# A head's row of score maxima written by one DMA from columns of every fourth query, without a transpose

## The reference

```python
# block 0: q = tgt @ Wq.T, k = memory @ Wk.T, v = memory @ Wv.T, 16 heads of 32
probs = jax.nn.softmax(einsum('bhqd,bhkd->bhqk', q, k) * scale, axis=-1)
att = einsum('bhqk,bhkd->bhqd', probs, v)
x = tgt + att[0]
# block 1, x (8, 512, 512), y (8, 512, 512)
q = layer_norm(x) @ Wq;  k, v = split(layer_norm(y) @ Wkv)
o = softmax(q k^T * 32 ** -0.5) v
x = x + o @ Wproj + bproj
x = x + gelu(layer_norm(x) @ W1 + b1) @ W2 + b2
```

## Time and profile before

| | us |
|---|---|
| median of 3 runs | 1885.43 |
| lowest and highest of them | 1879.63, 1895.04 |
| the profiled execution | 1889.92 |
| its span in the trace | 1888.1 |
| TensorE (PE) busy | 1750.5 (93%) |
| mean granted TensorE clock | 0.972 |

### The profile page before, as it was taken

One profiled execution on the slowest core, in us unless ns is written; L12 is line 12 of the kernel. 1 busy time (PEld: TensorE's weight loads), 2 busy tenths in 40 slices (PEclk: granted clock), 3 DMA queues, 4 the chain that ended last, 5 costly groups with the idle time before them and its releaser, 6 DMA issues.

```text
span 1888.1 us, 23894 instructions
## 1 busy us (share of the span) xinstructions
PE 1750.5 (93%) x7488; PEld 1339.1 (71%) x7488; DVE 1094.3 (58%) x1860; ACT 1166.9 (62%) x1935; POOL 935.6 (50%) x778
## 2 busy tenths in 40 slices
PE   6899999887898899999999999999999999999898
PEld 5677777655566677767667767777776677677687
DVE  4566655565676565756655655656566666654322
ACT  3677774677777666756756576667566565765231
POOL 0455422476764464546544554655455455546331
PEclk8999999999999999999999999999999999999999
DMA  6689945787545664675466455646654774557262
GB/s 231 220 286 294 310 173 177 270 276 237 183 125 176 162 185 132 189 201 165 141 201 182 143 157 172 197 126 186 205 160 138 211 187 143 157 168 243 81 237 89
DMA packets 156382, 354.69 MB, mean 188 GB/s; under 512 B 28512, under 2 KB 47072, under 8 KB 155360
## 3 DMA queue, kind: packets, MB, share of 16 engines
q1 hardware_dynamic: 125440, 240.95, 41.8%
q10 hardware_dynamic: 30816, 112.21, 19.1%
HBM read 251.51 MB, written 82.08 MB: 177 GB/s over the span
## 4 chain that ended last, share of the span: by engine, by line
PE 69%; ACT 8%; DVE 6%; DMA 6%; issue 5%; POOL 3%; SPq 3%; DVEq 0%; ACTq 0%; POOLq 0%
PE ps_d L862 46%; PE ps_o L911 11%; PE ps_t L894 5%; PE ps_s L879 5%; DMA q_st<-negmax_t 3%; SPq L637 2%; DVE negmax L1147 1%; ACT ps_d L927 1%; DMA k_st<-k_scratch 1%; PE ps_d L792 1%; DVE rs_t L1126 1%; ACT p_hi L1006 1%; ACT ps_t L1013 1%; ACT L1006 1%; DVE stats L1104 1%
## 5 line engine op out<-in xcount | busy, mean ns | idle before, releaser
L1257 POOL TENSOR_TENSOR p_lo<-p_full,p_hi 128x512 fp32r<-128x512 f32 x288 | 371.5, 1290 | 633.9 <-ACT p_full L1013 631.2
L1006 ACT ACTIVATE p_hi<-ps_t 128x512 fp32r<-128x512 f32 x576 | 345.2, 599 | 417.0 <-PE ps_t L894 416.1
L1147 DVE TENSOR_REDUCE negmax<-ps_s 128x1 fp32r<-128x512 f32 x576 | 389.9, 680 | 187.5 <-PE ps_s L879 187.2
L862 PE MATMUL ps_d<-hT,w_r 128*128 128x512 f32 x1536 | 432.3, 398 | 3.5 <-DVE hT L1052 1.8
L862 PE MATMUL ps_d<-w_r,g_s 128*128 128x512 f32 x1536 | 399.7, 398 | 5.5 <-DMA w_r<-w_scratch 5.5
L862 PEld LDWEIGHTS ps_d<-hT,w_r 128*128 128x128 f32 x1536 | 293.0, 191 | 81.7 <-DVE hT L1052 3.0
L862 PEld LDWEIGHTS ps_d<-w_r,g_s 128*128 128x128 f32 x1536 | 294.6, 192 | 77.2 <-issue 8.7
L1160 DVE TENSOR_TENSOR p_lo<-ps_t,p_hi 128x512 fp32r<-128x512 f32 x288 | 198.7, 690 | 231.4 <-ACT ps_t L1013 229.8
L911 PE MATMUL ps_o<-p_hi,v_s 128*65 128x512 f32 x576 | 236.6, 411 | 45.9 <-ACT o_raw L1029 40.9
L894 PE MATMUL ps_t<-q_st,k_st 97*128 97x512 f32 x576 | 235.8, 409 | 32.3 <-DMA q_st<-negmax_t 32.2
L879 PE MATMUL ps_s<-k_st,q_st 96*128 96x512 f32 x576 | 236.8, 411 | 11.3 <-DVE negmax L1147 9.6
(11 more groups left out here) (99 smaller groups left out, 2185.1 us busy)
## 6 DMA issues: line engine op xcount, KB each, us to landing
w_r<-w_scratch ACTq DMA_DIRECT2D x214, 512.0 KB, 5.1
w_r<-w_scratch SPq DMA_DIRECT2D x42, 512.0 KB, 4.7
v_scratch<-v_out SPq DMA_DIRECT2D x36, 520.0 KB, 3.9
v_s<-v_scratch SPq DMA_DIRECT2D x36, 520.0 KB, 5.2
k_scratch<-kq_out SPq DMA_DIRECT2D x36, 512.0 KB, 3.9
q_scratch<-kq_out SPq DMA_DIRECT2D x36, 512.0 KB, 3.3
q_st<-q_scratch SPq DMA_DIRECT2D x144, 128.0 KB, 4.3
k_st<-k_scratch SPq DMA_DIRECT2D x144, 128.0 KB, 4.3
```

The lines of the kernel that those rows point to most:

```text
L862: ins = nc.tensor.matmul(bank(u), lhs[a], rhs[b], start=(i == 0 and m == 0), stop=(i == 3 and m == 2))
L1006: act.activation(p_hi[:, c], ps_t[:, c % 2], ACT.Exp, scale=SCALE)
L1147: dve.tensor_reduce(negmax[:, h % 2, c:c + 1], ps_s[:, c % 2], AX.X, ALU.max, negate=True).then_inc(s_maxed, 1)
L1257: pool.tensor_tensor(p_lo[:, c], p_full[:, (by_gpsimd(s) - 1) % 2], p_hi[:, c].bitcast(F32), ALU.subtract).then_inc(p_pool_split, 1)
```

## The change

The first product takes as stationary operand, in place of 128 neighbouring queries, every fourth query, beginning with query c. So partition p of chunk c holds query 4 p + c, and the four columns of negmax hold on partition p the values of queries 4 p to 4 p + 3, which is the order of the row. One DMA with 128 pieces of 16 bytes writes the 2 KB row directly. The transposes, their buffer and their semaphore go, as does the clearing of negmax, which shrinks from 32 to 4 columns. The wait for the row of head h - 2 moves ahead of the first reduction of head h.

```diff
-ROW_DMAS = TC
+ROW_DMAS = 1
-    negmax = sb("negmax", [P, 2, 32], F32R)
-    negmax_t = sb("negmax_t", [P, 2, 32], F32)
+    negmax = sb("negmax", [P, 2, TC], F32R)
-    max_turned = sem("max_turned")
         def load_row(h):
-            sp.wait_ge(max_turned, h + 1)
-            for c in range(TC):
-                sp.dma_start(q_st[KQ:KM, h % G, c * P:c * P + P].bitcast(F32),
-                             negmax_t[c:P:32, h % 2]).then_inc(row_loaded[h % 2], 16)
+            sp.wait_ge(s_maxed, h * TC + TC)
+            sp.dma_start(q_st[KQ:KM, h % G].bitcast(F32), negmax[:, h % 2].bitcast(F32)).then_inc(row_loaded[h % 2], 16)
-                nc.tensor.matmul(ps_s[:, c % 2], q_st[0:KQ, h % G, c * P:c * P + P], k_st[0:KQ, h % G],
+                nc.tensor.matmul(ps_s[:, c % 2], q_st[0:KQ, h % G, c:T:TC], k_st[0:KQ, h % G],
                                  start=True, stop=True).then_inc(s_ready, 1)
-        dve.memset(negmax[:].bitcast(F32), 0.0)
-        dve.drain()
         for tick in range(TICKS):
             s = PLAN.s_at.get(tick)
             if s is not None:
                 h, c = divmod(s, TC)
+                if c == 0 and h >= 2:
+                    dve.wait_ge(row_loaded[h % 2], 16 * ROW_DMAS * (h // 2))
                 dve.wait_ge(s_ready, s + 1)
                 dve.tensor_reduce(negmax[:, h % 2, c:c + 1], ps_s[:, c % 2], AX.X, ALU.max,
                                   negate=True).then_inc(s_maxed, 1)
-                if c == TC - 1:
-                    dve.wait_ge(s_maxed, s + 1)
-                    if h >= 2:
-                        dve.wait_ge(row_loaded[h % 2], 16 * ROW_DMAS * (h // 2))
-                    dve.transpose(negmax_t[:, h % 2], negmax[:, h % 2].bitcast(F32)).then_inc(max_turned, 1)
```

## The result

The changed kernel takes 1864.28 us (median of 4 runs, 1860.23 to 1868.02), the kernel before 1889.13 us (4 runs, three of them those of the table above). The ratio is 0.986, 95% interval 0.982 to 0.991: some 25 us faster, a little over 1%. Over the 23 runs of the kernel before that stand beside the last experiments its median is 1886.38 us; by that one the change gives 22 us. The profiled execution has a span of 1858.4 us, against 1888.1. It is the fastest of its four runs and the one of before is slower than its median, so the 30 us between the two traces are some more than the change is worth.

A forecast was written before the change was run, and what follows sets the result against it. PE, busy 93% of the span, was taken as the bound, with row stalls costing at most 52 us. Terms -4 - 1 + 0 + 1 + 0 = -4 took 1889.9 to about 1886 profiled, 1881 as median; range 1850 to 1905.

The forecast's parts named there:

- A: PE's row stalls: they stay as long as their backlog, all else is hidden; 1881 us, within 1876 to 1889, chance 0.42.
- rival B: PE's row stalls: four small DMAs with completions were slow, so the stalls go; 1833 us, half 1859, chance 0.20.
- The sign that was given for A: PE's waits for the row stay near 12, 25 to 33 us in all, at the same 1 MB transfers.
- The fewer issues: SP: 432 of 576 row issues go; 0.3 us gained per stall, 4 us in all, at most 1.7 us each.
- The transposes: DVE: 30 us of its time goes and SP's wait starts 0.25 us sooner; 1 us gained.
- The moved wait on DVE: DVE's first reduction of a head: its wait for an earlier head's row never comes last; worth nothing.
- The packets: Row DMA: 112 more packets per head; 1 us lost at the 12 stalls, bounds 1 and 10 us.
- The strided load: PE's weight load of the scores: at least 77 ns to grow unseen, so zero; upper bound 60 us.
- rivals C and D: Strided weight load on PE: C, slower but nearly hidden, 1897 us, chance 0.18; D, exposed, 1941 us, chance 0.10.
- The sign that I gave for being right: PE's scores: strided weight loads recorded under 0.27 us, and the next load still 0.24 us later.
- Theory 2: From the experiments: at output stores, a row issued behind ACT's 0.5 MB weight load in the other queue waits for it too.

## Why the prediction was right, and where not

*The direction and the size.* Within 1% was the forecast (1881, range 1850 to 1905), and 1864 lies in the range, 22 to 25 us under the kernel before and at the edge of what can be told. That is owed to a wide range and not to the mechanism. 4 us were forecast, 1864 is outside A's own range (1876 to 1889), and it is nearer to half of rival B (1859). The sign that was given for A, a wait of 25 to 33 us, failed as well: 13.2.

*The fewer issues.* This is the term that was mis-sized. I took 0.3 us per stall, 4 us in all, since the four DMAs stood behind the same backlog. With the transposes kept, so that little but the row's DMA differs from the kernel before, the wait fell by 14.1 us and the time by 16. Of the whole change's 19.0 us of wait, 11.8 are at the six output stores, and there three stalls fell by 2.7 to 3.3 us, over the 1.7 that I had called the bound. The step that failed is that I took the backlog as fixed by what SP had issued ahead of the row. The 1.7 us of issuing reach past the moment at which ACT issues 0.5 MB in the other queue, and moving that load alone gave 7.9 us at these stores. I had the weight load in the same timelines and didn't set it against the row's issue. The longest stall, at 437 us, I misread too: "smaller transfers in the other queue" don't exist there. From 425 to 437 us all of it is SP's own queue:

```profile
q1 hardware_dynamic: 1671, 3.76, 90.7%
```

That is 3.76 MB where I counted 2.5; the rest are transfers that SP issued shortly before and behind the row.

*Rival B's reason* (four small DMAs, each with a completion) isn't needed for most of the gain at the stores: spare DMAs ahead of the row cost 15 us less of stall with the load out of the way. A part may remain. Also with the load out of the way the spare DMAs cost 12 us (1878.8 against 1866.6), and the row in four DMAs of 16-byte pieces waited 12 us more than in the four of the earlier trace rows.

*The transposes:* 1 us was forecast and 6 us measured. SP starts the row and the load of values behind it 0.25 us earlier each time (27 ns behind the last reduction at the median, against 273); that this is what gave the rest was not tested by itself.

*The moved wait on DVE:* nothing, as forecast. No wait of DVE for the row stands in the profile after.

*The packets:* 112 more per head, as counted from the earlier trace rows, and the DMA share of q1 went from 41.8% of 1888 us to 43.2% of 1858, 14 us of each engine's time. The stalls got shorter all the same, so the cost is below the gain; its size stays open, since the four DMAs of 16-byte pieces did worse than the four of before.

*The strided load:* zero was right, its reason half so. I thought that a load longer than 0.27 us would delay its matmul; 0.31 us doesn't. The longer load, 121 ns over 128 columns, agrees with the penalty that the Trainium skill names ("Advanced Engine Details and Errata", Memory Cachelines). No run used another stride, so it isn't shown that the line of 16 bytes is what costs. The size is near the doubled column of rivals C and D. They had the size and were wrong about its price: the overlap is larger than the earlier trace rows could show. The sign that I gave for being right, a load under 0.27 us, was the wrong one; the pace of the loads was the right one.

## What to carry to other kernels

When a small transfer is late behind large ones, compare the issue times of both queues around the stall before rewriting how it is made: here one 0.5 MB load moved by 2.35 us gave 19 us, and the rewriting gave 22. An engine that issues several small DMAs for one small result comes later to its next large load, here by half a microsecond for each; in this kernel that fell into the busiest moment. A weight load that is recorded as longer cost nothing here (309 ns at a pace of 234), since the next one started at the same pace.

## What was not expected

Spare DMAs behind the row slow it. With them the 520 KB load of values starts 4.5 us ahead of the output store instead of 6.5, and in three of six stores the row is in at 14 us rather than 11, though it was issued ahead of the weight load. In those three the last load of keys ahead of the row (issued at 3.7 to 4.1 us) lands at 13.4 to 14.6 us instead of 10.1 to 10.5. One of six stores in the run with the contiguous load did the same with no spare DMA (row in at 14.2, the others at 10.2 to 10.7), and so did the keys in four stores of the kernel before. The load of values starts some 4.5 us ahead of the store in the kernel before as well; but it does so too with the weight load one tick later, where no load of keys is late. So neither the weight load nor the late load of values does it alone in these runs; what tips the DMA engines from one outcome into the other is open.

7 us of the wait that went lie outside the six stores, all of them ahead of 500 us, where no weight load of ACT moves: 16.2 us of stalls before, 9.0 after. Theory 2 can't explain these. The runs that only move the weight load have there the same instructions as their kernel and show the scatter of one execution: 13.7 us for the kernel before, 7.4 and 12.4 for the changed one. So a gain is likely there, of some 5 us by the means (15.0 against 9.6), and its cause is open; that the row got faster in a queue of its own speaks for the backlog of SP's queue.
